# A graph-attention network on one core: another order of four engine queues inside a pipeline step, with the normalisation shift of a tile made in its own step

## Chip, cores, metric

One core of a Trainium2 chip. The metric is the device time of one execution in microseconds; the kernel before takes 1664.76 us, the median of 3 runs (1663.25 to 1664.78).

## What is computed

`x` holds 128 graphs of 64 nodes with 256 features, `adj` the edges of each graph. Two blocks follow each other, each with a residual:

```python
h = relu(layernorm(x))
# block one: graph attention with 8 heads of 32 features
xp = h @ W_proj                                   # (graph, node, 256)
a_src, a_dst = (xp per head) . W_att[:, :32], (xp per head) . W_att[:, 32:]
scores = leaky_relu(a_src[i] + a_dst[j] + b_att, 0.2); scores = -1e30 where there is no edge
x = x + relu(softmax(scores) @ xp)
# block two: three layers of one-head attention, layernorm, MLP (256 -> 1024 -> 256, gelu), layernorm
h = relu(layernorm(x))
x = x + three_layers(h, adj)
```

## The kernel before

Tokens lie on the 128 partitions, two graphs to a tile, so `x` is 64 tiles of 128 x 256. The program has two parts. The first (lines 100 to 560) does block one tile by tile; the second (from line 562) does block two, with groups of four tiles. Beside block one, the first part splits the weights of block two into a high and a low half: `w1` in 12 pieces during steps 2 to 13, and `w2` in 48 pieces, one in each step from 16 to 63. `w2` itself is loaded into the room of the raw `w1`, in three transfers that GpSimd issues in steps 5, 9 and 13, each after it has waited until VectorE has made the last low piece of that layer of `w1` (`s_wlo`).

Every engine runs the same steps, 0 to 73, written out by hand: a step works on a different tile for each stage, and an engine goes on to its next instruction only when the semaphore named in the wait has its count. Steps 16 to 63 are a loop on the engines whose body holds four steps. The order of the instructions within a step is the order in which `step(tau, t)` writes them, engine by engine. In step `tau` the stages are, with the tile in brackets:

- VectorE: `leaky` (tau-6, line 491), statistics `stats` of the incoming tile (tau, 496), `top` (tau-6, 503), `inv` of the head products (tau-8, 509), `stats` of the finished residual (tau-9, 512), `shifted` (tau-6, 516), `headout` (tau-8, 522), `no_edge` (tau-4, 528), the means and variances `mv` (531, 534) with `neg` and `vare` (538, 539), then `a_dst`, `src_hi`, `src_lo` (tau-4, 547 to 551).
- GpSimd: `rstd` and `nmr` (428, 430) of the statistics of step tau-1, the low half `w_lo` of a piece of `w2` (433), the load of `w2` (439), `x_res` = `headout` + `x` (tau-8, 446), the diagonals `dst_diag` (tau-4, 452, two halves).
- ScalarE: the high half `w_hi` of the piece (357), `hT` (tau-2, 362), `hrelu` (tau-1, 367, needs `nmr`), `xh` (tau-4, 376), `weights_T` (tau-7, 381), `x_act` (tau-10, 388, needs `nmr`), `scored` (tau-5, 395), the exponentials `weights` (tau-6, 400).
- TensorE: turning `hrelu` (tau-2, 286), the head products (tau-8, 300), turning `weights` (tau-7, 308), the projection `xp` (tau-3, 318), and the masked scores of tile tau-5 in one bank: `no_edge` (329), `src_hi` and `src_lo` (332), and `dst_diag` last (334).

Four of the waits matter below. `hrelu` waits for `nmr` of its tile. `xh` of tile T waits until the head products of tile T-4 are done (`q_ag`), which belong to the same step. `scored` waits for line 334 of the same tile. The exponentials wait for `shifted`, and the turning of a tile's `weights` waits for the exponentials of the step before.

Of the kernel before, what the change touches and what calls it, by code (L numbers as in the profile page):

```python
# [12 lines left out]
P = 128  # L13
# [5 lines left out]
def at_least(eng, sem, value):  # L19

    if not isinstance(value, int) or value > 0:
        eng.wait_ge(sem, value)
# [33 lines left out]
def graph_net(nc, x, adj, w_proj, w_att, b_att, attn_w, attn_b, w1, b1, w2, b2, g1, beta1, g2, beta2, out):  # L56
# [32 lines left out]
    with ctx:  # L89
# [23 lines left out]
        with first:  # L113
# [68 lines left out]

            def has(T):
                return not isinstance(T, int) or 0 <= T < NT

# [3 lines left out]
            def splits_w2(tau):  # L189
                return not isinstance(tau, int)  # L190
# [74 lines left out]
            def _(pe):  # L265
                def step(tau, t):
                    if isinstance(tau, int) and tau < 2 * L:
# [10 lines left out]
                        mm.then_inc(s_bias, 1)  # L278
                    T, r = tau - 2, (t - 2)
# [23 lines left out]
                    T, r = tau - 7, (t - 7)  # L303
                    if has(T):
                        pe.wait_ge(q_e, T + 1)
                        at_least(pe, q_ev, T)
                        for p in range(HP):
                            mm = pe.transpose(bank[5][:, p * P:(p + 1) * P], weights[:, p].rearrange("p e j -> p (e j)"), ident[:])
                        mm.then_inc(q_wt, 1)
                    T, r = tau - 3, (t - 3)  # L310
                    if has(T):
                        if isinstance(T, int) and T == 0:
                            pe.wait_ge(s_su, 2 * KD * 2)
                        pe.wait_ge(q_hT, T + 1)
                        at_least(pe, q_xh, T - 1)
                        at_least(pe, q_asd, 3 * (T - 1))
                        for k in range(KD):
                            mm = pe.matmul(bank[2 + r % 2][:, 0:WC], hT[:, r % 2, k * P:(k + 1) * P], wcat[:, k, :],
                                           start=(k == 0), stop=(k == KD - 1))
                        mm.then_inc(q_xp, 1)  # L320
                    T, r = tau - 5, (t - 5)
                    if has(T):
# [8 lines left out]
                        for a in (src_hi, src_lo):  # L331
# [3 lines left out]
                                  start=False, stop=True).then_inc(q_bc, 1)  # L335

# [3 lines left out]
            def _(act):  # L340
# [5 lines left out]
                def step(tau, t):  # L346
# [12 lines left out]
                    if has(T):  # L359
# [23 lines left out]
                    if has(T):  # L383
                        act.wait_ge(q_nmr, T + 10)

                        if r % 4 == 0:
# [3 lines left out]
                                       bias=nmr[:, (r + 1) % 4, 1:2], scale=rstd[:, (r + 1) % 4, 1:2]).then_inc(q_act, 1)  # L390
                    T = tau - 5
# [17 lines left out]
            def _(pool):  # L409
# [13 lines left out]
                def step(tau, t):  # L423
                    S, r = tau - 1, (t - 1)
# [36 lines left out]
            def _(dve):  # L461
# [24 lines left out]
                def step(tau, t):  # L486
# [31 lines left out]
                    if has(T):  # L518
# [658 lines left out]
```

## Time and profile before

| | |
|---|---|
| time, median of 3 runs | 1664.76 us |
| the profiled execution's own time | 1663.78 us |
| its span, first to last instruction | 1662.0 us |
| VectorE busy | 1378.4 us, 83% |
| TensorE busy (matmul) | 1524.7 us, 92% |
| ScalarE busy | 1087.1 us, 65% |
| GpSimd busy | 891.4 us, 54% |
| last instruction of the first part's VectorE steps | about 346 us |
| mean granted TensorE clock | 0.972 |

Busy time counts an engine while an instruction of it runs, and matmuls overlap their neighbours, so a start-to-start distance says more than a duration. An idle stretch is put down to the engine whose semaphore came last. The first part ends with a barrier of all engines, and the second starts behind it.

### The profile page before, as it was taken

Reading aid. Unit: us, or ns where it says so; the run is one execution under the profiler, and the core shown is the slowest. Engines: PE = TensorE matmul, PEld = TensorE weight load, DVE = VectorE, ACT = ScalarE, POOL = GpSimd, SP = SyncE. Lnnn points to the kernel's source line nnn. Section 1 sums busy time; section 2 is a strip of 40 time slices with the busy share of each in tenths; the row PEclk is TensorE's granted clock in tenths of the full one; section 3 lists DMA queues with packets and bytes.
Section 4 is the critical chain, followed back from the end, with each engine's and each line's share of the span. In section 5 each row is a group of like instructions: output and inputs, shape, how many; then the busy total and the mean of one; then the engine's idle time right before and its main releaser. Section 6 shows DMA issues by size and latency. Waiting matters only on the chain. (4 is left out here: it accounts for less than half of the span.)

```text
span 1662.0 us, 37278 instructions
## 1 busy us (share of the span) xinstructions
PE 1524.7 (92%) x11360; PEld 1282.6 (77%) x11360; DVE 1378.4 (83%) x4302; ACT 1087.1 (65%) x1946; POOL 891.4 (54%) x1008
## 2 busy tenths in 40 slices
PE   6888888827999999998999999899999999999995
PEld 6566666616888888887888888788888888888885
DVE  2889999967988989887888988888898888988852
ACT  1667777714677677665767666576777766677663
POOL 1667777723455355563545456444545656355464
PEclk9999999957999999999999999999999999999998
DMA  6233333250000011110001111100011211000001
GB/s 183 81 122 120 100 113 113 77 186 18 7 14 14 13 39 47 57 62 11 7 14 29 45 49 64 34 8 14 14 39 29 80 33 39 7 14 7 14 26 51
DMA packets 70894, 83.00 MB, mean 50 GB/s; under 512 B 29264, under 2 KB 54096, under 8 KB 70736
## 3 DMA queue, kind: packets, MB, share of 16 engines
q1 hardware_dynamic: 69104, 74.76, 15.2%
q0 software_dynamic: 816, 3.15, 0.6%
q10 hardware_dynamic: 816, 3.15, 0.5%
q8 instruction: 80, 1.31, 0.3%
q14 instruction: 78, 0.64, 0.1%
HBM read 38.95 MB, written 25.17 MB: 39 GB/s over the span
## 5 line engine op out<-in xcount | busy, mean ns | idle before, releaser
L805 ACT ACTIVATE bank<-bank,b_col 128x512 f32<-128x512 f32 x384 | 253.0, 659 | 365.2 <-PE bank L753 364.9
L765 PE MATMUL bank<-w_hi,hid_hi 128*128 128x256 f32 x1536 | 443.3, 289 | 17.8 <-DVE hid_lo L965 13.0
L765 PE MATMUL bank<-w_hi,hid_lo 128*128 128x256 f32 x1536 | 433.2, 282 | 0.0
L765 PE MATMUL bank<-w_lo,hid_hi 128*128 128x256 f32 x1536 | 432.8, 282 | 0.0
L965 DVE TENSOR_TENSOR hid_lo<-bank,hid_hi 128x512 fp32r<-128x512 f32 x384 | 259.1, 685 | 146.5 <-ACT hid_hi L810 143.0
L765 PEld LDWEIGHTS bank<-w_hi,hid_hi 128*128 128x128 f32 x1536 | 289.3, 188 | 53.8 <-DVE hid_lo L965 41.5
L753 PE MATMUL bank<-nT_hi,w_hi 128*128 128x512 f32 x768 | 318.2, 414 | 6.2 <-issue 4.8
L753 PE MATMUL bank<-nT_hi,w_lo 128*128 128x512 f32 x768 | 305.0, 397 | 4.8 <-issue 4.8
L753 PE MATMUL bank<-nT_lo,w_hi 128*128 128x512 f32 x768 | 304.0, 396 | 0.0
L765 PEld LDWEIGHTS bank<-w_lo,hid_hi 128*128 128x128 f32 x1536 | 289.6, 189 | 10.3
L765 PEld LDWEIGHTS bank<-w_hi,hid_lo 128*128 128x128 f32 x1536 | 289.4, 188 | 0.0
L924 POOL TENSOR_TENSOR rs_f<-ve_f,minus_half 128x4 f32<-128x4 f32 x48 | 48.9, 1018 | 423.8 <-DVE ve_f L994 423.8
L1008 DVE CUSTOM_DVE_ANT_0 dots<-x_cur,att_row 128x256 f32<-128x256 f32 x384 | 226.8, 591 | 14.1 <-DMA adj_raw<-in_adj_dram 4.0
L810 ACT CAST hid_hi<-bank 128x512 fp32r<-128x512 f32 x384 | 226.2, 589 | 13.2
L753 PEld LDWEIGHTS bank<-nT_hi,w_hi 128*128 128x128 f32 x768 | 146.0, 190 | 47.1 <-issue 28.6
L753 PEld LDWEIGHTS bank<-nT_hi,w_lo 128*128 128x128 f32 x768 | 145.4, 189 | 34.3
L753 PEld LDWEIGHTS bank<-nT_lo,w_hi 128*128 128x128 f32 x768 | 146.3, 190 | 17.8
L917 POOL TENSOR_TENSOR rs_a<-ve_a,minus_half 128x4 f32<-128x4 f32 x48 | 48.5, 1011 | 180.1 <-DVE ve_a L1084 180.1
L907 POOL TENSOR_TENSOR n_tok<-n_tok,g_row 128x512 f32<-128x512 f32 x96 | 122.6, 1301 | 15.7 <-PE bank L743 12.5
L911 POOL TENSOR_TENSOR n_tok<-n_tok,c_row 128x512 f32<-128x512 f32 x96 | 130.6, 1385 | 0.0
L815 ACT ACTIVATE y_tok<-y_tok,nm_f,rs_f 128x256 f32<-128x256 f32 x192 | 104.9, 597 | 10.0 <-POOL nm_f L926 9.6
L832 ACT ACTIVATE n_tok<-n_tok,nm_a,rs_a 128x256 f32<-128x256 f32 x192 | 99.8, 593 | 12.3 <-POOL nm_a L919 12.3
(122 smaller groups left out, 3076.9 us busy)
## 6 DMA issues: line engine op xcount, KB each, us to landing
x_other<-x_cur SPq DMA_DIRECT2D x96, 128.0 KB, 2.4
xin<-in_x_dram SPq DMA_DIRECT2D x16, 512.0 KB
first_block_out<-x_res SPq DMA_DIRECT2D x16, 512.0 KB
second_block_in<-x_act SPq DMA_DIRECT2D x16, 512.0 KB
x_cur<-second_block_in SPq DMA_DIRECT2D x16, 512.0 KB, 3.7
x_fin<-first_block_out SPq DMA_DIRECT2D x16, 512.0 KB, 3.6
out_dram<-x_fin SPq DMA_DIRECT2D x16, 512.0 KB, 2.9
xh_other<-xh SPq DMA_DIRECT2D x128, 33.0 KB, 1.9
```

Source lines behind the costliest of these rows:

```text
L753: mm = pe.matmul(HID[(CF * s + c) % 3][:], w[:, l, k, c * P:(c + 1) * P], a[:, s % 2, k, :], start=(k == 0 and p == 0), stop=(k == KD - 1 ...
L765: mm = pe.matmul(FF[t // 2][:, (t % 2) * D:(t % 2 + 1) * D], a[:, r, t * P:(t + 1) * P], w[:, l, c, :], start=(c == 0 and t % 2 == 0 and p ...
L805: act.activation(h[:], h[:], ACT.Gelu, bias=b1_col[:, l, c:c + 1]).then_inc(s_gelu, 1)
L810: act.copy(hid_hi[:, (CF * s + c) % HRING, :], HID[(CF * s + c) % 3][:]).then_inc(s_hi, 1)
L815: act.activation(y_tok[:, par, t, :], y_tok[:, par, t, :], ACT.Identity, bias=nm_f[:, t:t + 1], scale=rs_f[:, t:t + 1]).then_inc(s_yn, 1)
L832: act.activation(n_tok[:, s % 2, t, :], n_tok[:, s % 2, t, :], ACT.Identity, bias=nm_a[:, t:t + 1], scale=rs_a[:, t:t + 1]).then_inc(s_n, 1)
L907: pool.tensor_tensor(base[:, h], base[:, h], g1_row[:, l].unsqueeze(1).broadcast_to([P, TG // 2, D]), ALU.mult).then_inc(s_base, 1)
L911: pool.tensor_tensor(base[:, h], base[:, h], c1_row[:, l].unsqueeze(1).broadcast_to([P, TG // 2, D]), ALU.add).then_inc(s_base, 1)
L917: pool.tensor_tensor(rs_a[:], ve_a[:], minus_half[:], ALU.pow).then_inc(s_rsa, 1)
L924: pool.tensor_tensor(rs_f[:], ve_f[:], minus_half[:], ALU.pow).then_inc(s_rsf, 1)
L965: dve.tensor_tensor(hid_lo[:, r, :], HID[(CF * s + c) % 3][:], hid_hi[:, r, :].bitcast(F32), ALU.subtract).then_inc(s_split, 1)
L1008: dve.tensor_tensor_reduce(dots[:], x_cur[:, g, t, :], att_row[:, l, j, :], 1.0, 0.0, ALU.mult, ALU.add, dst[:, t:t + 1]).then_inc(s_dots, 1)
```

## The change

Only the first part is touched, and there only the order within a step. The instructions are the same ones.

- TensorE: turning `weights` (tau-7) comes first in the step, then turning `hrelu`, the head products, the masked scores, and `xp` last.
- ScalarE: `w_hi` and `hT` move from the front to behind `x_act`, in front of `scored`.
- GpSimd: the piece of `w_lo` comes first and now also waits for `shifted` of the step; `rstd` and `nmr` are made for the statistics of step tau, not tau-1, and so stand in front of the load of `w2`, of `x_res` and of the diagonals.
- VectorE: `headout` moves from behind `shifted` to behind `vare`.

```diff
@@ tensor @@
+                    T, r = tau - 7, (t - 7)
+                    if has(T):
+                        pe.wait_ge(q_e, T + 1)
+                        at_least(pe, q_ev, T)
+                        for p in range(HP):
+                            mm = pe.transpose(bank[5][:, p * P:(p + 1) * P], weights[:, p].rearrange("p e j -> p (e j)"), ident[:])
+                        mm.then_inc(q_wt, 1)
                     T, r = tau - 2, (t - 2)
...
                         mm.then_inc(q_ag, 1)
-                    T, r = tau - 7, (t - 7)
...
-                    T, r = tau - 3, (t - 3)
...
                     T, r = tau - 5, (t - 5)
...
                                   start=False, stop=True).then_inc(q_bc, 1)
+                    T, r = tau - 3, (t - 3)
...
@@ scalar @@
-                    if splits_w2(tau):
-                        act.copy(w2_part(w2_hi, tau), raw_part(tau)).then_inc(s_whi, 1)
-                    T, r = tau - 2, (t - 2)
-                    if has(T):
-                        act.wait_ge(q_tr, T + 1)
-                        at_least(act, q_xp, T - 1)
-                        act.copy(hT[:, r % 2, :], bank[r % 2][:, 0:D]).then_inc(q_hT, 1)
...
+                    if splits_w2(tau):
+                        act.copy(w2_part(w2_hi, tau), raw_part(tau)).then_inc(s_whi, 1)
+                    T, r = tau - 2, (t - 2)
...
@@ gpsimd @@
-                    S, r = tau - 1, (t - 1)
+                    if splits_w2(tau):
+                        pool.wait_ge(q_d, tau - 5)
+                        pool.wait_ge(s_whi, 4 * L + 1 + (tau - HEAD))
+                        pool.tensor_tensor(w2_part(w2_lo, tau), raw_part(tau),
+                                           w2_part(w2_hi, tau).bitcast(F32), ALU.subtract).then_inc(s_w2lo, 1)
+                    S, r = tau, t
                     if counted(S):
                         pool.wait_ge(q_mv, S + 1)
...
-                    if splits_w2(tau):
-                        pool.wait_ge(s_whi, 4 * L + 1 + (tau - HEAD))
-                        pool.tensor_tensor(w2_part(w2_lo, tau), raw_part(tau),
-                                           w2_part(w2_hi, tau).bitcast(F32), ALU.subtract).then_inc(s_w2lo, 1)
@@ vector @@
-                    if has(T):
-                        heads.wait()
-                        at_least(dve, q_res, T)
-
-                        heads.done(dve.scalar_tensor_tensor(headout[:].rearrange("p (h k) -> p h k", h=H), G[:, :, 0:HK],
-                                                            0.0, inv[:].unsqueeze(2).broadcast_to([P, H, HK]),
-                                                            ALU.max, ALU.mult))
...
                         dve.tensor_scalar(vare[:, t % 4].unsqueeze(2), mv[:, t % 4, :, 1:2], EPS, None, ALU.add).then_inc(q_mv, 1)
+                    T = tau - 8
+                    if has(T):
+                        heads.wait()
+                        at_least(dve, q_res, T)
+
+                        heads.done(dve.scalar_tensor_tensor(headout[:].rearrange("p (h k) -> p h k", h=H), G[:, :, 0:HK],
+                                                            0.0, inv[:].unsqueeze(2).broadcast_to([P, H, HK]),
+                                                            ALU.max, ALU.mult))
```

TensorE in the loop, before: from the turning of `weights` (`bank<-ident,weights`) to the first head product (`bank_7<-xh,weights_T`) of the next step.

```order
L308 MATMUL bank<-ident,weights 128x128 [waits q_weights_T_kept,q_weights]
L308 MATMUL bank<-ident,weights 128x128 x3
L318 MATMUL bank<-wcat,hT 128x272 [waits q_src_dst,q_xh,q_hT_kept]
L318 MATMUL bank<-wcat,hT 128x272
L329 MATMUL bank<-no_edge,ident_r 128x512 [waits q_score_steps,q_no_edge]
L332 MATMUL bank<-src_hi,ident_r 128x512 [waits q_src_dst]
L332 MATMUL bank<-src_lo,ident_r 128x512
L334 MATMUL bank<-dst_diag,same_graph 128x512 [waits q_diag]
L286 MATMUL bank<-ident,hrelu 128x128 [waits q_hT_kept,q_h]
L286 MATMUL bank<-ident,hrelu 128x128
L300 MATMUL bank_7<-xh,weights_T 64x33 [waits q_weights_T_kept,q_xh_other,q_heads_steps]
```

The same piece after the change, from the masked scores of one step to the first head product of the next; line numbers are those of the changed file.

```order
L318 MATMUL bank<-no_edge,ident_r 128x512 [waits q_score_steps,q_no_edge]
L321 MATMUL bank<-src_hi,ident_r 128x512 [waits q_src_dst]
L321 MATMUL bank<-src_lo,ident_r 128x512
L323 MATMUL bank<-dst_diag,same_graph 128x512 [waits q_diag]
L333 MATMUL bank<-wcat,hT 128x272 [waits q_src_dst,q_xh,q_hT_kept]
L333 MATMUL bank<-wcat,hT 128x272
L284 MATMUL bank<-ident,weights 128x128 [waits q_weights_T_kept,q_weights]
L284 MATMUL bank<-ident,weights 128x128 x3
L293 MATMUL bank<-ident,hrelu 128x128 [waits q_hT_kept,q_h]
L293 MATMUL bank<-ident,hrelu 128x128
L307 MATMUL bank_7<-xh,weights_T 64x33 [waits q_weights_T_kept,q_xh_other,q_heads_steps]
```

Between the turning of `weights` and the masked scores there stood the projection (`bank<-wcat,hT`); now the turning of `hrelu` and the head products stand there, and the projection comes behind `dst_diag`.

GpSimd in the loop, before: from the diagonals of one step to `x_res` of the next.

```order
L452 TENSOR_TENSOR dst_diag<-node_of,a_dst 128x256 [waits q_masked_spread]
L452 TENSOR_TENSOR dst_diag<-node_of,a_dst 128x256
L426 REGISTER_ALU
L428 TENSOR_TENSOR rstd<-vare,minus_half 128x2 [waits q_act,q_mean_var]
L430 TENSOR_TENSOR nmr<-neg,rstd 128x2 [waits q_rstd]
L432 REGISTER_ALU
L433 ISA [waits weight_hi]
L433 TENSOR_TENSOR w_lo<-raw_weights,w_hi 128x128
L443 ISA
L446 ISA [waits q_heads_steps]
L446 ISA
L446 TENSOR_TENSOR x_res<-headout,xin 128x256
```

After the change, one step up to the first half of its diagonals (REGISTER_ALU and ISA rows work out addresses).

```order
L426 REGISTER_ALU [waits q_shifted]
L427 ISA [waits weight_hi]
L427 TENSOR_TENSOR w_lo<-raw_weights,w_hi 128x128
L431 REGISTER_ALU
L22 REGISTER_ALU [waits q_mean_var]
L433 TENSOR_TENSOR rstd<-vare,minus_half 128x2 [waits q_act]
L435 TENSOR_TENSOR nmr<-neg,rstd 128x2 [waits q_rstd]
L444 ISA
L447 ISA [waits q_heads_steps]
L447 ISA
L447 TENSOR_TENSOR x_res<-headout,xin 128x256
L450 ISA
```

`rstd` and `nmr` of a step's own statistics now stand ahead of `x_res`; `w_lo` stands ahead of them, and its wait for `w_hi` (`weight_hi`) is joined by one for `shifted`.

ScalarE in the loop, before: from the register work behind `hT` to the exponentials.

```order
L365 REGISTER_ALU
L367 ISA [waits q_h_turned,q_shift]
L367 ACTIVATE hrelu<-xin,nmr,rstd 128x256
L22 REGISTER_ALU [waits q_heads,q_proj]
L376 COPY xh<-bank 128x8x32 [waits q_xh_other]
L381 COPY weights_T<-bank 128x512 [waits q_heads,q_weights_T]
L388 ISA [waits q_shift]
L388 ACTIVATE x_act<-x_res,nmr,rstd 128x256
L22 ISA [waits q_masked_spread]
L395 COPY scored<-bank 128x512 [waits q_score_steps]
L400 ACTIVATE weights<-shifted 128x2x4x64 [waits q_weights_T,q_shifted]
```

After the change, one step from `hrelu` on.

```order
L360 ACTIVATE hrelu<-xin,nmr,rstd 128x256
L22 REGISTER_ALU [waits q_heads,q_proj]
L369 COPY xh<-bank 128x8x32 [waits q_xh_other]
L374 COPY weights_T<-bank 128x512 [waits q_heads,q_weights_T]
L381 ISA [waits q_shift]
L381 ACTIVATE x_act<-x_res,nmr,rstd 128x256
L385 ISA
L385 COPY w_hi<-raw_weights 128x128
L390 COPY hT<-bank 128x256 [waits q_proj,q_h_turned]
L22 ISA [waits q_masked_spread]
L395 COPY scored<-bank 128x512 [waits q_score_steps]
L400 ACTIVATE weights<-shifted 128x2x4x64 [waits q_weights_T,q_shifted]
```

`w_hi` and `hT`, which came ahead of `hrelu`, now come between `x_act` and `scored`.

## Rows read from the trace of the kernel before

**Rows 1.** busy time in the stretch 60 to 100 us (microseconds, instructions, granted clock PEclk)
```profile
60.00:100.00 40.00, 32.33 (x320) 22.10 (x318) 30.69 (x109) 23.45 (x51) 23.55 (x38) 0.83 0.37 110
```

**Rows 2.** waits between 140 and 300 us: total, times, longest (us)
```profile
ACT hrelu L367 <- POOL nmr L430: 41.4, 36, 1.4
```

**Rows 3.** timeline of VectorE (start, duration): `leaky` of step 16 and step 64
```profile
99.76 0.69 DVE L491 SCALAR_TENSOR_TENSOR leaky<-bank,scored 128x512 f32<-128x512 f32 x1 [2.68 <-ACT scored L395]
...
315.28 0.69 DVE L491 SCALAR_TENSOR_TENSOR leaky<-bank,scored 128x512 f32<-128x512 f32 x1 [0.16 <-ACT scored L395]
```

**Rows 4.** timeline of TensorE in step 40 and the start of step 41
```profile
208.06 0.66 PE L308 MATMUL bank<-ident,weights 128*128 128x128 f32 x4 [0.19 <-ACT weights L400]
208.55 1.08 PE L318 MATMUL bank<-wcat,hT 128*128 128x272 f32 x4
209.27 0.59 PE L329 MATMUL bank<-no_edge,ident_r 128*128 128x512 f32 x1
...
210.13 1.02 PE L334 MATMUL bank<-dst_diag,same_graph 128*128 128x512 f32 x2
...
212.46 0.66 PE L308 MATMUL bank<-ident,weights 128*128 128x128 f32 x4 [0.30 <-ACT weights L400]
```

**Rows 5.** timeline of ScalarE in steps 39 and 40
```profile
205.66 0.35 ACT L376 COPY xh<-bank 128x256 f32<-128x256 f32 x1
...
206.90 0.58 ACT L395 COPY scored<-bank 128x512 f32<-128x512 f32 x1
...
207.89 0.30 ACT L357 CAST w_hi<-raw_weights  x1
...
211.29 0.59 ACT L395 COPY scored<-bank 128x512 f32<-128x512 f32 x1
211.77 0.63 ACT L400 ACTIVATE weights<-shifted 128x512 f32<-128x512 f32 x1
```

**Rows 6.** timeline of TensorE, turning of `hrelu` and head products of step 65
```profile
318.76 0.38 PE L286 MATMUL bank<-ident,hrelu 128*128 128x128 f32 x2
...
319.52 0.22 PE L300 MATMUL bank<-xh,weights_T 64*64 64x33 f32 x1
```

**Rows 7.** timeline of VectorE and GpSimd in step 41
```profile
215.20 0.72 POOL L446 TENSOR_TENSOR x_res<-headout,xin 128x256 f32 x1 [0.36 <-DVE headout L522]
215.22 0.72 DVE L539 TENSOR_SCALAR vare<-mv 128x2 f32<-128x2 f32 x1
```

**Rows 8.** all instructions of one line: ns min/median/max, first and last start
```profile
L539 DVE TENSOR_SCALAR vare<-mv x73: 154/164/740, 20.5 to 345.6; 128x2 f32<-128x2 f32 x73
...
L433 POOL TENSOR_TENSOR w_lo<-raw_weights,w_hi x48: 454/462/952, 100.7 to 312.7; - x48
```

**Rows 9.** timeline of GpSimd in step 40
```profile
208.29 0.70 POOL L428 TENSOR_TENSOR rstd<-vare,minus_half 128x2 f32<-128x2 f32 x1
209.07 0.20 POOL L430 TENSOR_TENSOR nmr<-neg,rstd 128x2 f32<-128x2 f32 x1
...
211.09 0.73 POOL L446 TENSOR_TENSOR x_res<-headout,xin 128x256 f32 x1 [1.33 <-DVE headout L522]
211.77 1.19 POOL L452 TENSOR_TENSOR dst_diag<-node_of,a_dst 128x256 f32<-128x256 f32 x2
```

**Rows 10.** timeline of three engines around the second load of `w2` (steps 9, 10)
```profile
63.34 0.96 POOL L439 DMA_DIRECT2D raw_weights<-in_L_gnn_W_dram  x1 [3.28 <-DVE w_lo L558]
...
66.75 1.13 PE L334 MATMUL bank<-dst_diag,same_graph 128*128 128x512 f32 x2 [2.00 <-POOL dst_diag L452]
67.68 0.60 ACT L367 ACTIVATE hrelu<-xin,nmr,rstd 128x256 f32<-128x256 f32 x1 [4.36 <-POOL nmr L430]
...
69.42 0.58 ACT L395 COPY scored<-bank 128x512 f32<-128x512 f32 x1
```

**Rows 11.** timeline of TensorE in step 5
```profile
40.74 2.02 PE L318 MATMUL bank<-wcat,hT 128*128 128x272 f32 x4
...
42.18 1.01 PE L329 MATMUL bank<-no_edge,ident_r 128*128 128x512 f32 x1
```

More of the change, by code:

```diff
@@ L302, in step @@
                         mm.then_inc(q_ag, 1)
-                    T, r = tau - 7, (t - 7)
-                    if has(T):
[L305 to L309, printed above, removed]
-                    T, r = tau - 3, (t - 3)
-                    if has(T):
[L312 to L320, printed above, removed]
                     T, r = tau - 5, (t - 5)
@@ L335, in step @@
                                   start=False, stop=True).then_inc(q_bc, 1)
+                    T, r = tau - 3, (t - 3)
+                    if has(T):
+                        if isinstance(T, int) and T == 0:
+                            pe.wait_ge(s_su, 2 * KD * 2)
+                        pe.wait_ge(q_hT, T + 1)
+                        at_least(pe, q_xh, T - 1)
+                        at_least(pe, q_asd, 3 * (T - 1))
+                        for k in range(KD):
+                            mm = pe.matmul(bank[2 + r % 2][:, 0:WC], hT[:, r % 2, k * P:(k + 1) * P], wcat[:, k, :],
+                                           start=(k == 0), stop=(k == KD - 1))
+                        mm.then_inc(q_xp, 1)
                 steps(pe, step)
@@ L355, in step @@
                                        scale=g1_col[:, l, q // 2:q // 2 + 1]).then_inc(s_whi, 1)
-                    if splits_w2(tau):
-                        act.copy(w2_part(w2_hi, tau), raw_part(tau)).then_inc(s_whi, 1)
-                    T, r = tau - 2, (t - 2)
-                    if has(T):
-                        act.wait_ge(q_tr, T + 1)
-                        at_least(act, q_xp, T - 1)
-                        act.copy(hT[:, r % 2, :], bank[r % 2][:, 0:D]).then_inc(q_hT, 1)
                     T, r = tau - 1, (t - 1)
@@ L390, in step @@
                                        bias=nmr[:, (r + 1) % 4, 1:2], scale=rstd[:, (r + 1) % 4, 1:2]).then_inc(q_act, 1)
+                    if splits_w2(tau):
+                        act.copy(w2_part(w2_hi, tau), raw_part(tau)).then_inc(s_whi, 1)
+                    T, r = tau - 2, (t - 2)
+                    if has(T):
+                        act.wait_ge(q_tr, T + 1)
+                        at_least(act, q_xp, T - 1)
+                        act.copy(hT[:, r % 2, :], bank[r % 2][:, 0:D]).then_inc(q_hT, 1)
                     T = tau - 5
@@ L517, in step @@
                                           ALU.subtract).then_inc(q_d, 1)
-                    if has(T):
-                        heads.wait()
-                        at_least(dve, q_res, T)
-                        heads.done(dve.scalar_tensor_tensor(headout[:].rearrange("p (h k) -> p h k", h=H), G[:, :, 0:HK],
-                                                            0.0, inv[:].unsqueeze(2).broadcast_to([P, H, HK]),
-                                                            ALU.max, ALU.mult))
                     T, r = tau - 4, (t - 4)
@@ L539, in step @@
                         dve.tensor_scalar(vare[:, t % 4].unsqueeze(2), mv[:, t % 4, :, 1:2], EPS, None, ALU.add).then_inc(q_mv, 1)
+                    T = tau - 8
+                    if has(T):
+                        heads.wait()
[3 more added lines that the diff above has]
+                                                            ALU.max, ALU.mult))
                     T, r = tau - 4, (t - 4)
```

## The prediction

> **What bounds the kernel now.** I first split the time into stretches. The change touches only the first part. Its loop runs from the `leaky` of step 16 at 99.76 us to that of step 64 at 315.28 us [rows 3]. That is 215.5 us for 48 steps, so 4.49 us a step. The rest of the first part is a head of 16 steps and a tail of 10. The second part keeps its instructions, so only the first can change, and the limit of the step has to be found.
>
> Then the waits inside the loop: the longest is that of ScalarE's `hrelu` for `nmr`, 41.4 us in 36 steps [rows 2], 1.15 us a step. It is no proof of a bound, since another chain could be just as long. So I followed rings, chains that return to their own start one or two steps later, through the timelines.
>
> *The ring of TensorE and ScalarE.* The turning of `weights` starts at 208.06, `xp` at 208.55, the masked scores at 209.27 and 210.13, where `dst_diag` takes 1.02 us until 211.15 [rows 4]. `scored` starts at 211.29, the exponentials at 211.77 [rows 5], and the next turning at 212.46 [rows 4]. Each follows the one before without a gap, and the ring closes in 4.40 us.
>
> *VectorE's lock.* In three steps of four, `vare`, an operation on two numbers a lane, takes 0.72 us instead of its median of 0.16 [rows 7, 8]. It starts at 215.22 while GpSimd's `x_res` runs from 215.20 to 215.92, and it ends with it. So 0.56 us x 3/4 = 0.42 us a step is lost on VectorE. This agrees with the Trainium skill ("SBUF — State Buffer", Who interferes with whom): the pair of ports that both engines use is an exclusive lock, and the second to come is blocked until the first is done.
>
> The step of 4.49 us is thus a little above a ring of 4.40, with VectorE and the wait for `nmr` close behind. Two limits of nearly one size mean that lifting one gives little.
>
> **The change, part by part.**
>
> *Head, the loads of `w2`.* GpSimd waits 3.28 us for VectorE, issues the load in 0.96 us, and only afterwards makes `x_res`, the diagonals and `nmr`; `hrelu` has by then waited 4.36 us, and `scored` starts at 69.42 [rows 10]. Now `nmr` stands ahead of the load. The diagonals don't: `dst_diag` on TensorE still ends at 66.75 + 1.13 = 67.88, and with the 0.14 us that `scored` needs behind it [rows 4, 5] it starts at 68.02. That is 1.4 us earlier. Steps 9 and 13 have this form (in step 5 no `scored` waits yet): -2.8 us. Its bounds are 0, if the wait moves to the head products, and twice that.
>
> *Head, first scores.* In step 5 `xp` runs at 40.74 and holds up the first masked scores until 42.18 [rows 11], 1.4 us. They now come first. `xp` itself comes later, and I keep -1.0 of it, between 0 and -1.4.
>
> *Loop, TensorE.* In the ring, `xp` (209.27 - 208.55 = 0.72 us) goes, and the turning of `hrelu` and the head products come in. Back to back these take from 318.76 to the last product's start at 319.52 [rows 6], 0.76, and about 0.05 until the next can start: 0.81. The ring becomes 4.40 - 0.72 + 0.81 = **4.49 us**. So the turning of `hrelu`, which the diff moves behind that of `weights` without naming it, costs as much as leaving out `xp` gives. TensorE has nothing to do while it waits for the exponentials, and before it did just these two things there.
>
> *Loop, GpSimd and VectorE.* `headout` and with it `x_res` come behind `vare`, so the lock of 0.42 us a step goes. Of the ring this takes nothing: `shifted` and `leaky` only come earlier than they are wanted. The longest wait, that of `hrelu`, goes too, and again another stands behind it. ScalarE's `xh` needs the head products of the same step, which used to run before the turning of `weights` and now run after it. A second ring appears, two steps long. Counted from the turning of `weights` (0): `hrelu` turned from 0.49, head products done at 0.49 + 319.74 - 318.76 = 1.47 [rows 6], `xh` at about 1.57. Then `xh`, `weights_T` and `x_act`, 206.90 - 205.66 = 1.24 [rows 5], `w_hi` at 2.81 and done at 3.11. `w_lo` waits for it and starts at about 3.36 (an estimate: 0.25, below the 0.36 that `x_res` idles before it starts [rows 7]), with 0.46 [rows 8] until 3.82. `rstd` until `nmr` 0.78, `nmr` 0.20, `x_res` 0.68, diagonals 1.19 [rows 9]: 6.67. Then `dst_diag` 6.73 to 7.75, `scored` 7.89, exponentials 8.37, next turning but one 9.06, by the distances of [rows 4, 5]. Half of it is **4.53 us**. Before, `w_lo` hung on no such chain.
>
> I take 4.52 us for the step, from these two: 48 x (4.52 - 4.49) = +1.4 us. The low end is 4.42 (the handoffs 0.1 shorter, and 0.05 less behind the head products), -3.4 us. The high end is 4.62, +6.2 us (the locks below).
>
> The lock is the place where a rule speaks against the change. In the trace, `w_lo` takes 0.46 us, and up to 0.95 when it meets `shifted` [rows 8]. By the Trainium skill ("SBUF — State Buffer", Who interferes with whom) an operation of VectorE with two inputs in SBUF, such as `shifted`, excludes one of GpSimd that reads SBUF, and whichever starts first holds the ports throughout; the diagonals, which now come 2 us behind `vare`, could hold up the next `shifted`. By the rows, the diagonals end at 6.67 in the count above. `shifted` follows the head products by about 0.5 us (an estimate), and those are done at 1.47 and one step later at 5.99; so it wants the ports at about 6.5, and the two overlap by 0.2 us. My sum leaves this out; with it on the two-step ring the step is 4.62.
>
> *Tail.* From step 66 on no `hrelu` is turned, from 67 on no `xp` made. Before, the loss of `xp` shortens the ring by 0.72 in three steps, 2.2 us; now the ring has lost `xp` already and gets 0.32 shorter in four steps, 1.3 us. The difference is +0.9, and about +0.1 for the later head products of the last tile: +1.0 us, between 0 and +3.
>
> *Sum.* -2.8 - 1.0 + 1.4 + 1.0 = **-1.4 us**. Against the profiled execution's own 1663.78 us this gives 1662.4; the median of the runs lies 1.0 above that execution, so I predict 1663.4 us. A measurement of this kernel can tell about 0.2%, 3.3 us, from no change. That is more than the sum.
>
> **The rivals.**
>
> *A, faster.* The step gets down to 4.42, because the handoffs of the second ring are shorter than put in, and TensorE keeps its clock in the head. Between 60 and 100 us the granted clock is 0.83 [rows 1], so for a third of that time it was at 1.2 GHz instead of 2.4, after the stretches in which TensorE waited for GpSimd [rows 10]. With shorter waits one or both falls may be gone, 1 to 2 us each. For it speaks that the 4.36 us wait surely goes. Against it: TensorE's own idle time of 2.00 us before `dst_diag` stays, since the diagonals are still behind the load. Worked out: -2.8 - 1.0 - 3.4 - 2.5 + 1.0 = -8.7, and with one fall left about -7: **1657.8 us**.
>
> *B, slower.* The two-step ring decides, with locks on it. When the diagonals and `shifted` meet, `w_lo`, which now waits for `shifted`, starts late, and all behind it: `rstd`, `nmr`, `x_res`, the diagonals, `dst_diag`. The place is GpSimd's queue; the price is 0.2 us per two steps, up to the 0.49 that such a meeting costs at most [rows 8]. Steps of 4.62 give +6.2 in the loop: -2.8 - 1.0 + 6.2 + 2 = +4.4, or **1669.2 us**. It decides from a step of about 4.58 on, where the loop has used up the head's gain and the bound of 0.2%. For it: a whole new chain hangs on `w_lo`. Against it: GpSimd itself is busy for only 3.3 us of the step.
>
> *C, VectorE was the bound.* Then the lock that goes, 0.42 us a step, would bring 20 us. The ring of 4.40 us without a gap speaks against it, and so does the new one of 4.49: no step can be shorter than that ring. I give it 0.02.
>
> **How the numbers follow.** My forecast (a step of 4.47 to 4.56, own range 1660.5 to 1667) gets 0.48, A 0.26, B 0.24, C 0.02. The range 1656.5 to 1670 holds A and B at their worked-out times and leaves out less than 0.2 at the ends. Faster by over 0.2% needs less than 1661.4: all of A and C and a small share of the forecast, 0.33. Slower, above 1668.1: B and a small share, 0.28. Within 0.2%: 0.39.
>
> **What would show it.** In the profile of the changed kernel the step should be 4.47 to 4.56 us. `vare` should take 0.16 us throughout. ScalarE's wait should no longer be `hrelu` for `nmr` in the head, and `xh` should wait for the head products. TensorE should start each turning of `weights` right behind the exponentials and run without a gap to the end of `dst_diag`. GpSimd's `w_lo` should wait for `w_hi`. In steps 10 and 14 `scored` should follow `dst_diag` at once. The forecast is wrong if the step falls below 4.42 (then something in the ring of TensorE is shorter than its rows say), if it is above 4.58 (locks or handoffs), or if the head gains more than 6 us.

## The result, and the profile after

| | before | after |
|---|---|---|
| time, median of 8 runs each | 1664.16 us | 1670.69 us (1668.40 to 1673.11) |
| ratio, 95% interval | | 1.0040 [1.0029, 1.0051] |
| span of the profiled execution | 1662.0 us | 1669.2 us |
| `leaky` of step 16 | 99.76 us | 92.97 us |
| `leaky` of step 64 | 315.28 us | 318.96 us |
| one step of the loop | 4.490 us | 4.708 us |
| last `x_act` ends | 347.43 us | 354.68 us |

The change made the kernel slower by 0.4%, and the time lies 0.7 us above the range. The forecast was 1663.4. From the last `x_act` to the end it is 1314.6 us before and 1314.5 after, so the whole difference of 7.2 us lies in the first part: **head -6.8, loop +10.5, tail +3.6**.

Timeline of VectorE after, where [rows 3] stand before:

```profile
92.97 0.69 DVE L492 SCALAR_TENSOR_TENSOR leaky<-bank,scored 128x512 f32<-128x512 f32 x1
...
318.96 0.69 DVE L492 SCALAR_TENSOR_TENSOR leaky<-bank,scored 128x512 f32<-128x512 f32 x1 [0.17 <-ACT scored L395]
```

The head, which answers to [rows 1] (columns: length, then busy time of PE, PEld, DVE, ACT, POOL, granted clock, DMA share, GB/s). TensorE was granted 1.00 between 60 and 100 us, where it had 0.83:

```profile
60.00:100.00 40.00, 34.33 (x394) 22.83 (x387) 35.07 (x127) 28.45 (x61) 26.97 (x44) 1.00 0.43 127
```

The waits between 140 and 300 us after (total, times, longest). Before, `hrelu` waited 41.4 us for `nmr` [rows 2]; now it waits 13.1, and as much waiting stands at `w_lo`, behind `w_hi`:

```profile
POOL w_lo L427 <- ACT w_hi L385: 42.8, 34, 1.5
ACT xh L369 <- PE bank L307: 21.8, 28, 1.0
...
PE bank L284 <- ACT weights L400: 14.1, 34, 0.5
ACT hrelu L360 <- POOL nmr L435: 13.1, 34, 0.5
PEld bank L323 <- POOL dst_diag L453: 8.1, 17, 0.5
```

The last row is new too: in every second of these 34 steps TensorE waits for the diagonals. Before, it never did in this stretch; `dst_diag` started 0.22 us behind `src_lo` in every step.

The long locks are gone: all instructions of `vare`, `shifted` and `w_lo` after (ns min/median/max), where [rows 8] had up to 740 and 952. What is left is small: in every second step the diagonals run 0.16 to 0.24 us into `shifted`, which then takes 0.71 to 0.79 us instead of 0.67.

```profile
L533 DVE TENSOR_SCALAR vare<-mv x73: 159/161/166, 20.1 to 352.8; 128x2 f32<-128x2 f32 x73
...
L517 DVE TENSOR_TENSOR shifted<-leaky,top x64: 651/675/792, 48.4 to 342.8; 128x512 f32<-128x512 f32 x64
...
L427 POOL TENSOR_TENSOR w_lo<-raw_weights,w_hi x48: 453/457/460, 96.9 to 318.2; - x48
```

The second ring of the prediction can be read off the timeline (three engines, in order of time):

```profile
201.70 0.66 PE L284 MATMUL bank<-ident,weights 128*128 128x128 f32 x4 [0.44 <-ACT weights L400]
...
202.95 0.22 PE L307 MATMUL bank<-xh,weights_T 64*64 64x33 f32 x1
...
203.37 0.37 ACT L369 COPY xh<-bank 128x256 f32<-128x256 f32 x1 [0.63 <-PE bank L307]
...
204.62 0.29 ACT L385 CAST w_hi<-raw_weights  x1
...
205.20 0.46 POOL L427 TENSOR_TENSOR w_lo<-raw_weights,w_hi  x1 [1.18 <-ACT w_hi L385]
...
205.61 0.70 POOL L433 TENSOR_TENSOR rstd<-vare,minus_half 128x2 f32<-128x2 f32 x1
...
206.39 0.19 POOL L435 TENSOR_TENSOR nmr<-neg,rstd 128x2 f32<-128x2 f32 x1
...
206.75 0.73 POOL L447 TENSOR_TENSOR x_res<-headout,xin 128x256 f32 x1 [0.16 <-issue]
...
207.43 1.19 POOL L453 TENSOR_TENSOR dst_diag<-node_of,a_dst 128x256 f32<-128x256 f32 x2
...
208.78 1.02 PE L323 MATMUL bank<-dst_diag,same_graph 128*128 128x512 f32 x2
...
209.93 0.59 ACT L395 COPY scored<-bank 128x512 f32<-128x512 f32 x1
...
210.42 0.63 ACT L400 ACTIVATE weights<-shifted 128x512 f32<-128x512 f32 x1
...
211.10 0.66 PE L284 MATMUL bank<-ident,weights 128*128 128x128 f32 x4 [0.39 <-ACT weights L400]
```

From 201.70 to 211.10 the chain runs through two steps: 9.40 us, 4.70 a step, where the prediction had put 9.06 together. Each row starts when the one above it allows, with one exception: `dst_diag` starts 0.22 us behind `src_lo`, its own predecessor on TensorE, and not at once behind the diagonals. In the neighbouring chain, which starts one step later, it is the diagonals that TensorE waits for:

```profile
206.57 0.65 PE L284 MATMUL bank<-ident,weights 128*128 128x128 f32 x4 [0.46 <-ACT weights L400]
...
208.56 0.38 PE L321 MATMUL bank<-src_lo,ident_r 128*128 128x512 f32 x1
...
212.32 1.18 POOL L453 TENSOR_TENSOR dst_diag<-node_of,a_dst 128x256 f32<-128x256 f32 x2
...
213.55 0.30 PEld L323 LDWEIGHTS bank<-dst_diag,same_graph 128*128 128x128 f32 x2 [0.52 <-POOL dst_diag L453]
...
215.97 0.66 PE L284 MATMUL bank<-ident,weights 128*128 128x128 f32 x4 [0.37 <-ACT weights L400]
```

That chain takes 9.40 us as well, and no link in it is loose. So the turnings of `weights` follow each other after 4.57, 4.87, 4.53 and 4.87 us, over and over: the short steps are those of the ring of TensorE and ScalarE, and the long ones are those in which the two-step chain arrives late. A ring of one step would give no such alternation by itself.

### The profile page after: what moved, and what is told of

Same layout as the page of the kernel before. It is cut to its first block and busy times, and to the rows that moved or that the text cites. A ratio compares the mean times of both kernels' runs of the same rounds, so it can differ in the third digit from the quotient of the medians.

```text
span 1669.2 us, 37302 instructions
## 1 busy us (share of the span) xinstructions
PE 1534.5 (92%) x11360; PEld 1271.9 (76%) x11360; DVE 1364.7 (82%) x4302; ACT 1095.0 (66%) x1946; POOL 877.6 (53%) x1008
```

## The experiments

Theory: the two-step ring sets the step. TensorE's new order puts the head products behind the turning of `weights`, and a chain from them through `rstd`, `nmr`, `x_res` and the diagonals closes two steps later. Rivals: locks of VectorE and GpSimd; a ring of one step. Below, "step" is the mean step of the loop in us (before 4.49, after 4.71), and each ratio is to the kernel before on the same chip.

**heads_first.** TensorE makes the head products ahead of the turning of `weights`, all else as changed:

```diff
-TensorE: weights turned, hrelu turned, head products, masked scores, xp
+TensorE: hrelu turned, head products, weights turned, masked scores, xp
```

> The changed kernel, with TensorE's step in the order: turning of hrelu, head products, turning of weights, masked scores, xp. Theory 1 (the two-step ring of 9.40 us in the changed kernel's trace, 4.70 a step, over turning of weights, head products, xh, x_act, w_hi, w_lo, rstd, nmr, x_res, diagonals, dst_diag, scored, exponentials sets the step): the head products leave the ring, xh no longer waits for them, and the step falls from 4.71 to 4.2 to 4.5 us; the whole takes 1655 to 1660 us. Theory 2 (the locks between the diagonals and shifted set it) and theory 3 (the new wait of w_lo for shifted sets it): the step stays at 4.65 to 4.75.

Measured: 1660.34 us, ratio 0.9982 [0.9972, 0.9991], step 4.54. Moving one piece of TensorE's queue takes the loss away and makes a version faster than both kernels. Its limit is another one. VectorE and GpSimd in step 40 of that kernel:

```profile
205.56 1.04 DVE L517 TENSOR_TENSOR shifted<-leaky,top 128x512 f32<-128x512 f32 x1
...
206.97 0.43 DVE L533 TENSOR_SCALAR vare<-mv 128x2 f32<-128x2 f32 x1
```

```profile
202.94 0.70 POOL L433 TENSOR_TENSOR rstd<-vare,minus_half 128x2 f32<-128x2 f32 x1 [0.18 <-DVE vare L533]
...
204.87 1.19 POOL L453 TENSOR_TENSOR dst_diag<-node_of,a_dst 128x256 f32<-128x256 f32 x2
206.90 0.48 POOL L427 TENSOR_TENSOR w_lo<-raw_weights,w_hi  x1 [0.84 <-DVE shifted L517]
207.56 0.70 POOL L433 TENSOR_TENSOR rstd<-vare,minus_half 128x2 f32<-128x2 f32 x1 [0.19 <-DVE vare L533]
```

The diagonals hold up `shifted` until they end at 206.06, `shifted` (1.04 instead of 0.67) holds up `w_lo` by the new wait, `w_lo` holds up `vare` (0.43 instead of 0.16), and `rstd` waits for `vare`. From `rstd` to `rstd` it is 4.62 us in this step: a ring of one step over the ports. Its steps no longer alternate between a short and a long one (4.53, 4.49, 4.62, 4.53).

**pe_only.** The kernel before, with TensorE's new order alone.

```diff
-TensorE: hrelu turned, head products, weights turned, xp, masked scores
+TensorE: weights turned, hrelu turned, head products, masked scores, xp
```

> The kernel before with only the change's order on TensorE. Theory 1: xh waits for the head products here too, and scored and w_hi stand behind it, while nmr is still late: the loop is slower than the kernel before, 4.6 to 4.85 us a step, 1670 to 1680 us. If the order on TensorE were harmless, the step would stay at 4.49 and the time at 1664.

Measured: 1680.31 us, ratio 1.0098 [1.0082, 1.0115], step 4.83. The TensorE part of the change costs 0.34 us a step by itself, more than the whole change (0.22). Which ring sets the 4.83 was not followed.

**w_lo_last** and **w_hi_front.** Each cuts the route over ScalarE's high half. The first puts `w_lo` behind the diagonals on GpSimd, the second puts `w_hi` back to the front on ScalarE.

```diff
 GpSimd (w_lo_last):  -w_lo  rstd nmr x_res dst_diag +w_lo
 ScalarE (w_hi_front): +w_hi hrelu xh weights_T x_act -w_hi hT scored weights
```

> The changed kernel, with w_lo at the end of GpSimd's step, behind the diagonals. Theory 1: w_lo no longer stands between w_hi and rstd, so the two-step ring is cut and the ring of TensorE and ScalarE is left, about 4.5 us: the loop takes 8 to 10 us less, 1661 to 1663 us in all. Theory 2 (locks): the diagonals still meet shifted, the step stays above 4.65. Theory 3 (wait for shifted): also falls to about 4.5.

> The changed kernel, with w_hi at the front of ScalarE's step again (hT stays where the change put it). Theory 1: the piece of w_hi no longer waits for xh; w_lo starts when shifted is done, 0.3 us or more earlier in every step, and the two-step ring shrinks: 4.5 to 4.6 us a step, 1662 to 1666 us. Theory 3 (the wait of w_lo for shifted): no change, 4.7. Theory 2 (locks): no change.

Measured: w_lo_last 1666.96 us, ratio 1.0021 [1.0011, 1.0030], step 4.65; w_hi_front 1671.24, ratio 1.0044 [1.0027, 1.0061], step 4.72. Both miss: the theory had expected about 4.5 in the first and 4.5 to 4.6 in the second, and cutting this route alone brings 0.05 us or nothing. VectorE in the first of them tells why:

```profile
204.61 0.21 DVE L510 RECIPROCAL inv<-bank 128x8 f32<-128x8 f32 x1
205.00 0.43 DVE L513 BATCH_NORM_STATS2 stats<-x_res 128x6 f32 x1 [0.18 <-issue]
205.34 0.71 DVE L517 TENSOR_TENSOR shifted<-leaky,top 128x512 f32<-128x512 f32 x1
...
206.42 0.17 DVE L533 TENSOR_SCALAR vare<-mv 128x2 f32<-128x2 f32 x1
```

```profile
206.75 0.70 POOL L428 TENSOR_TENSOR rstd<-vare,minus_half 128x2 f32<-128x2 f32 x1 [1.24 <-DVE vare L533]
```

A second route leads from the same head products over `inv`, `stats`, `shifted` and `vare` to the same `rstd`, and is only some 0.1 us shorter.

**both_cut.** TensorE's new order stays; both routes are cut. VectorE's new order also needs a wait of `leaky` for the `shifted` of the step before, which is in this version and in hf_vare_early.

```diff
 GpSimd:  -w_lo  rstd nmr x_res dst_diag +w_lo
-VectorE: leaky stats(x) top inv stats(x_res) shifted no_edge mv neg vare headout
+VectorE: leaky stats(x) top stats(x_res) mv neg vare inv shifted no_edge headout
```

> The changed kernel, TensorE's order kept (head products behind the turning of weights), with both routes from the head products to rstd cut at once: the low half stands behind the diagonals on GpSimd (cuts the route over ScalarE's high half), and on VectorE the means, neg and vare are made ahead of inv, from the stats of the finished residual that stand there too (cuts the route over inv, stats and shifted). Theory of the two parallel two-step routes: cutting one gave 4.65 instead of 4.71 us, cutting both leaves the route inv, shifted, headout, x_res, about 8.2 us long, and TensorE's one-step ring of 4.53 decides: 4.53 to 4.60 us a step, 1660 to 1664 us. Rival (something else makes TensorE's new order slow, such as the head products coming late for the step itself): 4.65 to 4.72 us, 1666 to 1671 us.

Measured: 1659.83 us, ratio 0.9985 [0.9975, 0.9995], step 4.58. The step is what the two-step theory said (4.53 to 4.60), with TensorE's order untouched: that order costs through the rings that it closes over the other engines. The alternation is gone as well (4.64, 4.56, 4.56, 4.57). What is left is the first ring of the prediction, with no gap in it. TensorE of that kernel:

```profile
205.50 0.66 PE L284 MATMUL bank<-ident,weights 128*128 128x128 f32 x4 [0.39 <-ACT weights L400]
...
206.90 0.50 PE L318 MATMUL bank<-no_edge,ident_r 128*128 128x512 f32 x1
...
207.67 1.02 PE L323 MATMUL bank<-dst_diag,same_graph 128*128 128x512 f32 x2
...
210.06 0.66 PE L284 MATMUL bank<-ident,weights 128*128 128x128 f32 x4 [0.44 <-ACT weights L400]
```

4.56 us against the 4.49 of the prediction.

**diag_first** and **hf_diag_first.** The diagonals ahead of `x_res` on GpSimd, in the changed kernel and in heads_first.

```diff
 GpSimd: w_lo rstd nmr -x_res dst_diag +x_res
```

> The changed kernel with GpSimd's diagonals made ahead of x_res in the step. Theory of the two-step routes (the head products behind the turning of weights start several routes to the diagonals, each 9.3 to 9.4 us long): x_res and its wait leave the piece between nmr and the diagonals on all of them at once, 0.68 to 1.0 us, so they shrink to about 8.5 and the one-step ring of TensorE, 4.53 us, decides: a step of 4.53 to 4.60 instead of 4.70, 1663 to 1666 us. Theory of the locks (the slower step is made by operations of VectorE and GpSimd that meet): the same instructions still share the ports, so the step stays at 4.65 to 4.75 and the time at 1668 to 1672 us. If instead the finished residual on VectorE (stats of x_res) comes too late, the step is above 4.75.

> The version with the head products first, and GpSimd's diagonals ahead of x_res. Theory of the port ring: the ring keeps its parts, since x_res now stands where the diagonals stood and meets shifted in their place: 4.45 to 4.60 us a step, 1657 to 1663 us. Rival (in that version the way over the diagonals, dst_diag and scored sets the step, not the ports): the diagonals come 0.7 to 1.0 us earlier, and the step falls to 4.3 to 4.4, 1650 to 1655 us.

Measured: 1689.38 us (ratio 1.0153 [1.0133, 1.0174]) and 1689.51 (1.0152 [1.0129, 1.0176]), a step of 5.085 in both. Neither of the main expectations held; the third case of the first one did. The two agree to 0.1 us although TensorE's order differs, so TensorE is on no ring that decides here. GpSimd and VectorE of diag_first:

```profile
213.11 0.72 POOL L455 TENSOR_TENSOR x_res<-headout,xin 128x256 f32 x1
```

```profile
214.13 0.43 DVE L513 BATCH_NORM_STATS2 stats<-x_res 128x6 f32 x1 [0.95 <-POOL x_res L455]
214.47 0.67 DVE L517 TENSOR_TENSOR shifted<-leaky,top 128x512 f32<-128x512 f32 x1
```

`shifted` stands behind the `stats` of `x_res`, `w_lo` waits for `shifted`, and `rstd`, `nmr`, the diagonals and `x_res` follow on GpSimd: a one-step ring that the late `x_res` makes longer. It says nothing on the two-step ring.

**old_pe.** The change without its TensorE part.

```diff
-TensorE: weights turned, hrelu turned, head products, masked scores, xp
+TensorE: hrelu turned, head products, weights turned, xp, masked scores
```

> The change without its TensorE part: GpSimd, ScalarE and VectorE in the new order, TensorE in the order of before (turning of hrelu, head products, turning of weights, xp, masked scores). Theory of the two-step routes: they all begin with head products that stand behind the turning of weights, so none is left; the ring of TensorE with xp in it (4.40 us) or the port ring (4.5 to 4.6) decides: 4.45 to 4.58 us a step, a head shorter by 3 to 7 us, 1656 to 1662 us. Rival (the new order of the other three engines is itself slower in the loop): above 4.62 us a step and above 1665 us.

Measured: 1658.82 us, ratio 0.9966 [0.9956, 0.9976], step 4.54, and `leaky` of step 16 8.9 us earlier than before, more than the 3 to 7 expected. The rest of the change is a gain of 0.3%, all of it in the head; next to it, TensorE's part costs 4.71 - 4.54 = 0.17 us a step.

**no_wait.** The changed kernel without the new wait.

```diff
-                        pool.wait_ge(q_d, tau - 5)
```

> The changed kernel without the new wait of GpSimd's low half for shifted. Theory: the low half starts when the high half is there (42.8 us of its waiting is for it), so the wait costs nothing here: 4.69 to 4.71 us a step, 1669 to 1672 us. Rival (the wait for shifted is what makes the change slower): a step of 4.50 to 4.60, below 1665 us.

Measured: 1672.35 us, ratio 1.0046 [1.0030, 1.0063], step 4.71. The step is as expected: the wait costs nothing while the two-step ring decides. (Its head is 2.2 us longer, with the granted clock at 0.91 between 60 and 100 us, although up to step 16 the two kernels have the same instructions: the wait stands only in the loop.)

**pow_twice** and **no_wait_pow_twice.** One more `pow` on GpSimd, into a spare tile, with and without that wait.

```diff
+                        pool.tensor_tensor(spare[:, r % 4, :], vare[:, r % 4, :], minus_half[:, 0:2], ALU.pow)
                         pool.tensor_tensor(rstd[:, r % 4, :], vare[:, r % 4, :], minus_half[:, 0:2], ALU.pow).then_inc(q_rs, 1)
```

> The changed kernel with GpSimd's pow of rstd done once more into a spare tile, 0.70 us busy and up to 0.78 from start to start, between vare and nmr. A ring of two steps through rstd grows by it once in two steps: +0.35 to +0.39 us a step, 5.06 to 5.10, and 1686 to 1691 us. Rival (a ring of one step through rstd): +0.70 to +0.78 a step, 5.40 and more, above 1702 us. Rival (rstd is on no ring that decides): less than +0.1 a step, below 1677 us.

> The changed kernel without the wait of the low half for shifted (1672 us, 4.71 us a step, so the wait cost nothing there) and with the pow of rstd done once more, 0.68 us from start to start. With the wait, the extra pow gave 5.20 us a step; read as the port ring, one step long, having taken over (4.54 + 0.68 = 5.22). Without the wait that ring is open, and only the two-step ring is left to grow: 4.71 + 0.34 = 5.05 us a step (5.03 to 5.09), about 1688 us (1685 to 1692). Rival (the ring through rstd in the changed kernel is one step long and the 5.20 had nothing to do with the wait): 5.18 us and more, above 1697 us.

Measured: 1700.97 us (ratio 1.0223 [1.0206, 1.0240]), step 5.20; and 1695.82 (1.0196 [1.0177, 1.0214]), step 5.14. For 0.68 us of work the step grows by 0.50 and 0.43: between the half of a two-step ring and the whole of a one-step ring, and outside what was expected. In the first, from `spare` to `spare` GpSimd shows the port ring, 5.20 us, as 4.54 + 0.68 would give:

```profile
208.69 0.70 POOL L433 TENSOR_TENSOR spare<-vare,minus_half 128x2 f32<-128x2 f32 x1 [0.18 <-DVE vare L534]
...
213.23 0.48 POOL L427 TENSOR_TENSOR w_lo<-raw_weights,w_hi  x1 [0.84 <-DVE shifted L518]
213.89 0.70 POOL L433 TENSOR_TENSOR spare<-vare,minus_half 128x2 f32<-128x2 f32 x1 [0.19 <-DVE vare L534]
```

In the second the wait is gone, but VectorE shows the ports still closing a ring of one step:

```profile
206.99 1.04 DVE L517 TENSOR_TENSOR shifted<-leaky,top 128x512 f32<-128x512 f32 x1
```

The diagonals run into `shifted`, which therefore ends at 208.03 only, `vare` stands behind it at 208.53, and the next `spare` starts at 208.85, 5.15 us behind the one before. By these timelines another ring, which was shorter than the two-step ring until 0.68 us was put into it, has taken over in both runs. So neither measures what it was made for. That the ring of the changed kernel is two steps long rests on its timeline, on the alternation of its steps, and on both_cut.

**hf_no_wait**, **hf_w_lo_last**, **hf_vare_early.** From heads_first: without the wait; then with `w_lo` behind the diagonals too; then also with VectorE's order of both_cut.

```diff
 hf_no_wait, GpSimd:     -wait for shifted
 hf_w_lo_last, GpSimd:   -w_lo  rstd nmr x_res dst_diag +w_lo
-hf_vare_early, VectorE: leaky stats(x) top inv stats(x_res) shifted no_edge mv neg vare headout
+hf_vare_early, VectorE: leaky stats(x) top stats(x_res) mv neg vare inv shifted no_edge headout
```

> The changed kernel with the head products put first on TensorE (the version that took 1660 us and 4.54 us a step), and without the wait of GpSimd's low half for shifted. Theory of the port ring (diagonals hold up shifted, shifted holds up the low half by that wait, and so rstd, nmr, x_res and the next diagonals, 4.62 us): the ring is opened, the step falls to 4.30 to 4.45 and the time to 1649 to 1656 us. Rival (TensorE and ScalarE set the step there, and the wait only hides in it): 4.52 to 4.56 us a step, 1659 to 1662 us. A third way: the low half now meets shifted and holds it up by 0.3 us in each step; then 4.6 and more, above 1663 us.

> The version with the head products first and without the wait for shifted (1653 us, 4.42 us a step), with the low half behind the diagonals on GpSimd. There VectorE works without a gap through most of the step, and only the diagonals that hold up shifted (0.97 to 1.06 us instead of 0.67) are lost on it. Theory: rstd waits for vare alone and comes 0.1 to 0.3 us earlier, the diagonals with it, shifted is held up less: 4.30 to 4.40 us a step, 1647 to 1652 us. Rival (the low half then meets shifted itself and takes what was won): 4.40 to 4.50, 1652 to 1657 us.

> Head products first on TensorE, no wait for shifted, the low half behind the diagonals, and the means, neg and vare ahead of inv on VectorE. Theory (in the version of 1653 us VectorE is held up by the diagonals that meet shifted, and rstd waits for a vare that stands behind shifted): rstd comes about 1 us earlier, though it may itself be held up by shifted as in the version with both routes cut (1.07 us), and the diagonals end before the next shifted wants the ports: 4.30 to 4.45 us a step, 1647 to 1654 us. Rival (TensorE and ScalarE form a ring of 4.5 us also with the head products first, which the version of 1653 us escaped by nothing but its own order): 4.50 to 4.58, 1657 to 1661 us.

| | time | ratio, 95% interval | step |
|---|---|---|---|
| hf_no_wait | 1652.95 us | 0.9938 [0.9919, 0.9957] | 4.42 |
| hf_w_lo_last | 1657.71 us | 0.9962 [0.9948, 0.9977] | 4.53 |
| hf_vare_early | 1639.65 us | 0.9866 [0.9847, 0.9885] | 4.19 |

The first opened the port ring, as expected. The second missed, and its rival's mechanism was right but too small: GpSimd starts `w_lo` at once behind the diagonals, meets `shifted`, and holds up `no_edge` (0.44 us instead of 0.18) and `vare` behind it.

```profile
213.20 1.06 DVE L516 TENSOR_TENSOR shifted<-leaky,top 128x512 f32<-128x512 f32 x1
214.18 0.44 DVE L521 TENSOR_SCALAR no_edge<-adjin 128x64 fp32r x1
```

```profile
213.67 0.90 POOL L453 TENSOR_TENSOR w_lo<-raw_weights,w_hi  x1
```

The third went below its expectation, to 1.3% under the kernel before. There the diagonals and `w_lo` are over before `shifted` starts; it is now `rstd` that is held up, which hurts less. GpSimd, and `shifted` at 208.12:

```profile
205.98 1.19 POOL L448 TENSOR_TENSOR dst_diag<-node_of,a_dst 128x256 f32<-128x256 f32 x2
207.12 0.46 POOL L453 TENSOR_TENSOR w_lo<-raw_weights,w_hi  x1
208.24 1.14 POOL L428 TENSOR_TENSOR rstd<-vare,minus_half 128x2 f32<-128x2 f32 x1 [0.65 <-DVE vare L518]
```

```profile
208.12 0.69 DVE L528 TENSOR_TENSOR shifted<-leaky,top 128x512 f32<-128x512 f32 x1
```

How much of its gain over hf_w_lo_last is the lock and how much the earlier `vare` was not separated.

## Why the prediction was wrong

**The step that failed** is "I take 4.52 us for the step", the term +1.4 us of the sum; it measured +10.5. The mechanism stood in the text, the second ring of two steps, and the instructions in it have the predicted durations. What was too small are the handoffs between them. A handoff is the time from the end of one instruction to the start of the next that waits for it. Start of each in the count of the prediction, from the turning of `weights`, for the two chains shown above:

| | predicted | chain from 201.70 | added at this link | chain from 206.57 | added at this link |
|---|---|---|---|---|---|
| `xh` | 1.57 | 1.67 | 0.10 | 1.64 | 0.07 |
| `w_lo` | 3.36 | 3.50 | 0.04 | 3.41 | -0.02 |
| `rstd` | 3.82 | 3.91 | -0.05 | 3.82 | -0.05 |
| `x_res` | 4.80 | 5.05 | 0.16 | 5.06 | 0.26 |
| `dst_diag` on TensorE | 6.73 | 7.08 | 0.10 | 6.99 | 0.00 |
| turning but one | 9.06 | 9.40 | -0.01 | 9.40 | 0.08 |

Together 0.34 us in each, 0.17 a step, 8 us in the loop. The largest part is `x_res`: in the loop it starts 0.16 to 0.27 us behind the end of `nmr`, and the prediction put this at nothing. The rows did not show it: before, `w_lo` stood between the two, and the 0.36 us of [rows 7] end with VectorE's `headout`; the prediction took a hint from them for `w_lo` and none for `x_res` itself. The 0.10 at `dst_diag` in the first chain is the queue of TensorE, as said above, and no handoff. The remaining 0.01 a step is the choice between 4.49 and 4.53 where the longer one decides. To choose between two rings is wrong: the step is at least the longest ring, and each handoff left out of it makes the sum too short. The head's error of -3.0 us made good a third of the loop's, so the total looks nearer than the terms were.

**The other ring** measured 4.56 instead of 4.49 (both_cut): the head products hold up the masked scores by 0.10 more than put in, `dst_diag` comes 0.09 sooner behind `no_edge`, and 0.06 lies at `scored` and the turning. "As costly as leaving out `xp` gives" was right to 0.07 us. At 4.58 a step it is still slower in the loop than the 4.49 before, so by this ring too TensorE's part gives nothing there.

**The lock** went as predicted, and so did the absence of a gain from it. The prediction's doubt whether the diagonals would meet `shifted`, by about 0.2 us, was answered by the changed kernel with yes, in every second step: diagonals until 204.02 and `shifted` at 203.85, but diagonals until 208.62 and `shifted` at 208.87. It lengthens `shifted` by 0.04 to 0.12 us, and `w_lo` is there later than `vare` all the same (in the chain shown, `vare` ends at 205.10 and `w_lo` holds GpSimd until 205.66), so none of it gets into the ring. With a shorter step they meet by 0.5 us (heads_first). This agrees with the Trainium skill ("SBUF — State Buffer", Who interferes with whom): the lock delays whichever comes second, `shifted` there, `no_edge` in hf_w_lo_last, `rstd` in hf_vare_early. Rival B named the two-step ring and nearly the time (1669.2), but put its price down to locks, and these cost the ring nothing: it came near by luck.

**The head** was -6.8 us, or -7.8 counted from the first `leaky`; the terms gave -3.8. The load of `w2` gave what was put in: the intervals behind steps 10 and 14 went from 7.08 and 7.07 us to 5.57 and 5.58, 1.5 each against 1.4. The rest lies in the intervals behind them, 6.35 to 5.02 and 6.86 to 4.51, where before the granted clock was 0.62 and 0.58; this is the part that rival A had and the forecast left out. What spoke against A, TensorE's idle time before `dst_diag` behind a load, did stay (up to 1.6 us), and the clock was 1.00 all the same. Four kernels have the same instructions up to step 16: the changed one, w_lo_last, w_hi_front and no_wait. From the first `leaky` to that of step 16 the first three took 46.3, 46.2 and 46.5 us at a clock of 1.00, and no_wait took 48.6 at 0.91. So a clock of 0.91 in the head goes with about 2.2 us, and 0.83 by the same measure with about 4.2 (an estimate from these runs: the time at the lower level is 0.17/0.09 as long), about what was missing (7.8 - 3.8 = 4.0). That the slower clock is the cause and not a companion of the longer head is not shown. The term for the first scores can't be judged: the first `leaky` starts anywhere from 43.6 to 47.8 us over the 16 kernels profiled here, which hides 1 us.

**The tail** was +3.6 instead of +1.0, above its bound of +3. The steps from 67 on stay at 4.18 us, where before they fell to 3.91 and 3.59; and from the last `leaky` to the end of the last `x_act` it takes 14.27 us instead of 11.75, for which the prediction had allowed 0.1. In pe_only that way takes 12.61 and in heads_first 13.22, so neither part of the change makes it alone, but the two together, 0.86 and 1.47, come near to the 2.52. In both_cut it takes 13.20. Which wait it is was not tried.

**Signs of the prediction:** `vare` at 0.16, `xh` waiting for the head products, `w_lo` for `w_hi`, the turning right behind the exponentials, `scored` 0.04 us behind `dst_diag` in steps 10 and 14: all came. One did not: TensorE should have run without a gap to the end of `dst_diag`, and in every second step it waits there for the diagonals. The step above 4.58 and the head above 6 us were the two signs it named for being wrong.

## What to carry to other kernels

An order within a step is judged by its rings, over as many steps as it takes to close one, and the longest decides: write all of them down, several often share their end, and cutting one alone then shows nothing. Sum a new ring with the handoffs that the trace shows for the same instructions (here 0.22 to 0.29 us from the end of `w_hi` to `w_lo`, 0.05 from the end of the diagonals to TensorE), and put a price on pairs that did not stand together before (here 0.16 to 0.27 from `nmr` to `x_res`), since each one left out errs to the same side. In this kernel, TensorE's work that waits for the last result of the previous step belonged behind the head products that were ready (heads_first), even though TensorE is idle in between.

## What was not expected of the hardware

On GpSimd `x_res` starts 0.36 us behind the start of `nmr` (206.39 to 206.75), which itself lasts 0.19, though nothing that it waits for is late; in other steps it is 0.46. And the granted clock in the head (60 to 100 us) was 0.83 before and 0.91 in pe_only; in the fourteen kernels with the new order on the other three engines it was 1.00 in eight, 0.96 in four and 0.91 in two. Order is not all of it, since among the four with the same instructions up to step 16 it was 1.00 three times and 0.91 once. The two intervals in which it had been down before became 3.7 us shorter, about as much as the whole head of the prediction.
